# Projection and routing of a transformer layer on one core: modulation moved to ScalarE behind the transposition, and GpSimd's work put in another order

## The reference

```python
x = x + ga * attention(...)
h = _layernorm(x, axis=-1) * (1 + cb) + sb
logits = h @ gate_w.T
scores = sigmoid(logits)
topk_idx, topk_w = route_tokens(scores, bias_corr)
shared = relu2(h @ shared_up_w.T) @ shared_down_w.T
```

## Time and profile before

| what | value |
|---|---|
| median of 3 runs | 2968.14 us (2962.25 to 2969.26) |
| profiled execution, span from its first to its last instruction | 3027.5 us |
| mean granted clock of TensorE in it | 0.985 |
| PE busy | 2895.4 us, 96% |
| VectorE busy | 2179.3 us, 72% |
| GpSimd busy | 1833.5 us, 61% |
| ScalarE busy | 1341.6 us, 44% |

### The profile page before, as it was taken

One profiled execution on the slowest core, in us unless ns is written; L12 is line 12 of the kernel. 1 busy time (PEld: TensorE's weight loads), 2 busy tenths in 40 slices (PEclk: granted clock), 3 DMA queues, 4 the chain that ended last, 5 costly groups with the idle time before them and its releaser, 6 DMA issues.

```text
span 3027.5 us, 49806 instructions
## 1 busy us (share of the span) xinstructions
PE 2895.4 (96%) x16480; PEld 2168.3 (72%) x16480; DVE 2179.3 (72%) x5344; ACT 1341.6 (44%) x2436; POOL 1833.5 (61%) x1077
## 2 busy tenths in 40 slices
PE   8999999999999999999999989999999999989997
PEld 5788888766666666666666677777777787767775
DVE  6555555678787878787877687777777787756664
ACT  2222222156666666666666522233222333226664
POOL 1233222278888888888886256766565666655664
PEclk9999999999999999999999999999999999999998
DMA  7655555756655665566555333332322322238996
GB/s 240 211 187 201 187 180 180 233 114 136 137 124 115 138 138 121 115 139 140 119 117 160 107 97 93 94 112 74 103 79 93 102 85 81 73 107 222 239 245 118
DMA packets 281948, 420.53 MB, mean 139 GB/s; under 512 B 48463, under 2 KB 132687, under 8 KB 281742
## 3 DMA queue, kind: packets, MB, share of 16 engines
q1 hardware_dynamic: 259214, 384.22, 44.9%
q0 software_dynamic: 22528, 33.72, 5.8%
HBM read 263.38 MB, written 153.01 MB: 138 GB/s over the span
## 4 chain that ended last, share of the span: by engine, by line
PE 53%; DVE 14%; POOL 14%; issue 8%; ACT 4%; DMA 4%; another core or an unknown queue 2%; DVEq 1%; POOLq 0%; SPq 0%; ACTq 0%
PE qkv_ps_m L840 12%; PE ffn_ps_m L2191 11%; POOL att_gathered L1105 6%; PE qkv_ps_m L844 6%; POOL att_pt L1098 5%; PE att_ps_o L1330 5%; PE att_ps_p L1386 4%; PE att_ps_s L1304 4%; DMA out<-exp_y,exp_tok_add 2%; PE exp_ps_u L1607 2%; PE exp_ps_y L1623 1%; PE att_ps_s L1361 1%; DVE ffn_att L147 1%; DVE ffn_x L149 1%
## 5 line engine op out<-in xcount | busy, mean ns | idle before, releaser
L247 DVE CUSTOM_DVE_ANT_0 att_ps_s<-att_ps_s,att_causal 128x512 f32<-128x512 f32 (+1 forms) x992 | 469.3, 502 | 175.5 <-PE att_ps_s L1304 171.3
L1166 ACT ACTIVATE att_pt<-att_ps_p 128x512 f32<-128x512 f32 (+1 forms) x1024 | 524.5, 589 | 143.6 <-PE att_ps_p L1389 110.2
L1304 PE MATMUL att_ps_s<-att_ks,att_qs 96*128 96x512 f32 x1488 | 513.4, 373 | 2.2 <-DVE att_lower L253 0.6
L1386 PE MATMUL att_ps_p<-att_qs,att_ks 98*128 98x512 f32 (+3 forms) x1536 | 498.5, 364 | 9.3 <-ACT att_pt L1166 8.0
L1098 POOL TENSOR_TENSOR att_pt<-att_pt 128x1024 f32<-128x1024 f32 (+2 forms) x153 | 331.1, 2164 | 166.6 <-PE att_ps_o L1330 144.8
L1105 POOL TENSOR_TENSOR att_gathered<-att_gathered,att_pt 128x2048 f32<-128x2048 f32 (+1 forms) x92 | 388.1, 4218 | 7.2
L1912 POOL DMA_INDIRECT slot_info<-ffn_info,ffn_slot x256 | 275.9, 1078 | 119.3 <-issue 76.5
L253 DVE TENSOR_REDUCE att_lower<-att_ps_s 128x1 f32<-128x512 f32 x496 | 339.2, 684 | 7.4 <-PE att_ps_s L1304 7.4
L1386 PEld LDWEIGHTS att_ps_p<-att_qs,att_ks 98*128 98x128 f32 x1536 | 272.6, 191 | 82.1 <-issue 34.7
L1304 PEld LDWEIGHTS att_ps_s<-att_ks,att_qs 96*128 96x128 f32 x1488 | 275.7, 191 | 73.3 <-DVE att_rowmax L247 27.7
L577 POOL TENSOR_TENSOR qkv_x<-qkv_x,qkv_mod 128x512 f32<-128x512 f32 x60 | 83.4, 1391 | 371.5 <-DVE qkv_x L671 371.5
(11 more groups left out here) (311 smaller groups left out, 6718.8 us busy)
## 6 DMA issues: line engine op xcount, KB each, us to landing
att_qs<-qk_parts SPq DMA_DIRECT2D x96, 512.0 KB, 6.8
att_ks<-qk_parts SPq DMA_DIRECT2D x96, 512.0 KB, 12.7
qk_parts<-qkv_out_hi SPq DMA_DIRECT2D x128, 256.0 KB, 2.2
qk_parts<-qkv_out_lo SPq DMA_DIRECT2D x128, 256.0 KB, 2.4
qkv_x<-x SPq DMA_DIRECT2D x16, 1024.0 KB, 5.6
v_rows<-qkv_out_v SPq DMA_DIRECT2D x64, 256.0 KB, 2.3
att_vs<-v_rows SPq DMA_DIRECT2D x32, 512.0 KB, 16.1
o_parts<-att_o SPq DMA_DIRECT2D x64, 256.0 KB, 7.9
```

The lines of the kernel that those rows point to most:

```text
L247: dve.tensor_tensor_reduce(part, part, self.causal[:, UNIT - (c1 - c0):UNIT], scale=1.0, scalar=MASKED, op0=ALU.add, op1=ALU.max, accum_ou ...
L1166: act.activation(tile(c)[:, h, col:UNIT], ps_p[(NPROB * prev.g + n) % NP][:, col:UNIT], ACT.Exp, scale=float(HD) ** -0.5).then_inc(exp_don ...
L1304: pe.matmul(bank("s", cur.g, i)[:, 0:c1 - c0], qs[cur.slot][0:STACK, h, t * P:(t + 1) * P], ks[cur.slot][0:STACK, h, c0:c1], start=True, s ...
L1386: last = pe.matmul(part[:, i * (UNIT - col):(i + 1) * (UNIT - col)], ks[prev.slot][:, h + i, kt * P:(kt + 1) * P], qs[prev.slot][:, h + i, ...
```

## The change

- `turn` on PE transposes the normalised, not yet modulated h2 (it waits for norm_done). TURNS puts transpositions 0 and 1 after tile 1 of the down projection, 2 after tile 2, and 3 before pair 2 of tile 3 instead of before pair 4.
- ScalarE scales and shifts each transposed tile in its PSUM bank, in four instructions of 128x128 with a scale and a bias per partition, from a new buffer `mod_cols`, and takes the high part afterwards. Two DMAs of 512 single elements each fill `mod_cols`.
- GpSimd modulates all four tiles of h2 itself (for the store, which the experts' gathers read), each after its transposition. Its order becomes: wait for all four norms, `normalise`, then four times a modulation of one tile of u + 1 and four scatters of u.
- VectorE no longer modulates tile 3. `norm_first` takes two instructions a tile instead of three.
- SP stores h2 of unit u in body u instead of body u - 1, and loads the modulation rows and columns behind it, in odd bodies, ahead of attention's output.

```diff
             def norm_first():
...
                 for t in range(UT):
-                    last = dve.tensor_scalar(late.h2[:, t, :], late.x0[:, t, :], bridge.mv[:, t, 0:1], bridge.rstd[:, t:t + 1],
-                                             ALU.subtract, ALU.mult)
+                    dve.scalar_tensor_tensor(late.h2[:, t, :], late.x0[:, t, :], bridge.mv[:, t, 0:1], bridge.mod[:, 1, :],
+                                             op0=ALU.subtract, op1=ALU.mult).then_inc(late.mul_done, 1)
...
-        TURNS = ((), (0,), (1, 2), ())
-        SCATTERED_AHEAD = TOPK
+        TURNS = ((), (0, 1), (2,), ())
+        LAST_TURN = 2
...
             def load_mod(b):
...
+                for m, j in enumerate((M_CB, M_SB)):
+                    sp.dma_start(mod_cols[:, m, :], mod_dram[bass.ds(b, 1), j, :].rearrange("o (k p) -> p (o k)", p=P),
+                                 allow_slow_non_contiguous=True).then_inc(mod_in, 16)
...
             def store_h2(b, half):
                 u = b * HALVES + half
-                sp.wait_ge(h_done, CREDIT + PT * (u + 1))
-                sp.wait_ge(norm_done, CREDIT + UT * (u + 1))
+                sp.wait_ge(h_done, CREDIT + UT * (u + 1))
...
-                if more:
-                    nb, nhalf = (b, 1) if half == 0 else (b + 1, 0)
...
-                        sp.wait_ge(proj_done, CREDIT + UT * (u + 2))
-                        load_o(b + 1, half)
-                    store_h2(nb, nhalf)
-                    if half == 0 and has_next2:
-                        load_mod(b + 1)
+                if u and more:
+                    store_h2(b, half)
+                if more and half == 1:
+                    sp.wait_ge(hi_done, CREDIT + UT * (u + 1))
+                    load_mod(b + 1)
+                if b < LAST:
+                    sp.wait_ge(proj_done, CREDIT + UT * (u + 2))
+                    load_o(b + 1, half)
...
+            def modulate(u, t):
+                pool.wait_ge(tr_done, CREDIT + UT * u + t + 1)
+                ht = h2[:, t, :]
+                pool.tensor_tensor(ht, ht, mod[:, 1, :], ALU.mult).then_inc(mul_done, 1)
+                pool.wait_ge(mul_done, CREDIT + UT * u + t + 1)
+                pool.tensor_tensor(ht, ht, mod[:, 2, :], ALU.add).then_inc(h_done, 1)
...
             def body(b, half, more):
                 u = b * HALVES + half
-                if u == UNITS - 2:
-                    scatter(u, half, 0, SCATTERED_AHEAD)
-                if more:
-                    modulate(*((b, 1) if half == 0 else (b + 1, 0)))
-                if half == 0 and not (isinstance(b, int) and b == LAST) or half == 1 and more:
-                    normalise(u + 2)
-                scatter(u, half, SCATTERED_AHEAD if u == UNITS - 2 else 0, UT * TOPK)
+                if b < LAST:
+                    pool.wait_ge(norm_done, CREDIT + UT * (u + 1))
+                    normalise(u + 2)
+                if more:
+                    pool.wait_ge(mod_in, CREDIT + MOD_FIRST + MOD_EACH * ((u + 1) // HALVES + 1))
+                    pool.sem_inc(mark, 1)
+                for t in range(UT):
+                    if more:
+                        modulate(u + 1, t)
+                    scatter(u, half, t * TOPK, (t + 1) * TOPK)
...
             def turn(u):
+                if u:
+                    act.wait_ge(mod_in, CREDIT + MOD_FIRST + MOD_EACH * (u // HALVES + 1))
                 for t in range(UT):
                     act.wait_ge(tr_done, CREDIT + UT * u + t + 1)
+                    if u:
+                        for k in range(DK):
+                            part = ps_t[t % 2][:, k * P:(k + 1) * P]
+                            last = act.activation(part, part, ACT.Identity, bias=mod_cols[:, 1, k:k + 1], scale=mod_cols[:, 0, k:k + 1])
+                        last.then_inc(modulated, 1)
+                        act.wait_ge(modulated, CREDIT + UT * (u - 1) + t + 1)
...
             def attend(b, half):
...
-                dve.wait_ge(mod_in, CREDIT + 48 * (b + 2))
+                dve.wait_ge(mod_in, CREDIT + MOD_FIRST + MOD_EACH * (b + 1))
...
-                dve.tensor_tensor(h2[:, PT, :], h2[:, PT, :], mod[:, 1, :], ALU.mult).then_inc(dve_own, 1)
-                dve.wait_ge(dve_own, own + 2)
-                dve.tensor_tensor(h2[:, PT, :], h2[:, PT, :], mod[:, 2, :], ALU.add).then_inc(norm_done, 1)
...
             def turn(u, t):
-                if t < PT:
-                    pe.wait_ge(h_done, CREDIT + PT * u + t + 1)
+                if u:
+                    pe.wait_ge(norm_done, CREDIT + UT * (u - 1) + t + 1)
```

More of the change, by code:

```diff
@@ L131, in __init__ @@
         self.tr_done, self.hi_done, self.lo_done = s.sem("tr"), s.sem("hi"), s.sem("lo")
+        self.modulated = s.sem("modulated")
         self.cross_done, self.logit_done = s.sem("cross"), s.sem("logit")
@@ L197, in __init__ @@
         self.q_in, self.v_in, self.m_in = s.sems("q_in", SLOT), s.sems("v_in", SLOT), s.sems("m_in", SLOT)
-        self.pool_own, self.add_done, self.sum_done, self.mark = (s.sem(n) for n in ("pool_own", "add", "sum", "mark"))
+        self.pool_own, self.add_done, self.sum_done = (s.sem(n) for n in ("pool_own", "add", "sum"))
+        self.mark = late.mark
         self.s_done, self.max_done = s.sem("s"), s.sem("max")
@@ L1246, in normalise_first @@
                 dve.wait_ge(late.x_in[0], CREDIT + 16)
-                dve.wait_ge(late.mod_in, CREDIT + 48)
+                dve.wait_ge(late.mod_in, CREDIT + MOD_FIRST)
             def norm_first():
@@ L1711, in project_programs @@
         mul_done, h_done, proj_done, att_done = late.mul_done, late.h_done, late.proj_done, late.att_done
-        tr_done, hi_done, lo_done = late.tr_done, late.hi_done, late.lo_done
+        tr_done, modulated, hi_done, lo_done = late.tr_done, late.modulated, late.hi_done, late.lo_done
         cross_done, logit_done = late.cross_done, late.logit_done
@@ L1839, in load_experts @@
                     relay.load_up(sp, e, e, e_upT)
+                store_h2(LAST, 1)
                 for e in range(RELAY_RING):
@@ L1866, in gpsimd @@
             pool.iota(tok_i[:, :], pattern=[[P, UT]], base=0, channel_multiplier=1).then_inc(pool_own, 1)
-            def modulate(b, half):
-                u = b * HALVES + half
-                for t in range(PT):
-                    pool.wait_ge(norm_done, CREDIT + UT * u + t + 1)
-                    ht = h2[:, t, :]
-                    pool.tensor_tensor(ht, ht, mod[:, 1, :], ALU.mult).then_inc(mul_done, 1)
-                    pool.wait_ge(mul_done, CREDIT + PT * u + t + 1)
-                    pool.tensor_tensor(ht, ht, mod[:, 2, :], ALU.add).then_inc(h_done, 1)
+            def modulate(u, t):
[4 more added lines that the diff above has]
+                pool.tensor_tensor(ht, ht, mod[:, 2, :], ALU.add).then_inc(h_done, 1)
             def normalise(u):
@@ L2020, in attend @@
                 late.deviation(dve, u, LINKS * u, mv, std, rstd, tmp)
-                own += 2 * UT + 1 + STAT_LINKS + ROOT_LINKS
                 dve.wait_ge(tr_done, CREDIT + UT * u)
@@ L2287, in before_pair @@
                     def before_pair(n):
-                        if more and t == PT and 2 * n == UP:
+                        if more and t == PT and n == LAST_TURN:
                             turn(u + 1, PT)
```

37 lines of the change are left out of this document (9 added, 28 removed).

## The result

| | before | changed |
|---|---|---|
| median of the timed runs | 2968.7 us (2962.25 to 2974.15, 4 runs) | 3042.8 us (3035.88 to 3055.25, 4 runs) |
| ratio, 95% interval | | 1.0251 (1.0222 to 1.0279) |
| span of the profiled execution | 3027.5 us | 3053.5 us |
| unit 0's to unit 15's last gate matmul | 956.2 us | 975.5 us |
| predicted | | 2988 us, 2942 to 3020 |

The change costs 74 us, not 20. The time is outside the range, on the side that I had called likeliest. The first thing to see is that the two profiled executions differ by 26 us only.

A forecast was written before the change was run, and what follows sets the result against it. PE, nearly always busy in the stage, can win only time it stands still or runs slow. Terms -45.3 + 55 + 8 + 3 - 1 = +20 on the 3027.5 us span, less 59, gave 2988 us, range 2942 to 3020.

The forecast's parts named there:

- Waits removed: PE's transposition waits for GpSimd's shift and hT_lo: 33.4 us go, with 11.9 us of lower clock, -45.3 us.
- The odd bodies: Modulation rows load late, delaying VectorE's update and PE's transposition: 9.2 us in each of six bodies, +55 us.
- The lower clock: PE's granted clock falls after the idle stretch before the down projection in odd bodies: 1.1 us a body.
- Even bodies: GpSimd's modulations run beside VectorE's choose steps and last a_lo: 1 us on each of eight, +8 us.
- ScalarE: Four more 278 ns instructions a tile, covered by 4.1 us of matmuls: cost nothing, 15 us at the upper end.
- GpSimd: Timetable in a body: normalise ends +1.0, modulate(0) +4.1, slots about +5.0, last modulated tile +31 us.
- The first norms' -1: First norms in the last attention group take 8 instructions instead of 12, mostly under PE's work: -1 us.
- The tail: Last unit: scatter(14), now with modulations between its parts, ends beside VectorE's choose steps: +3 us (0 to 5).
- Faster: Rival: slots at +3, rows at +35.9, odd bodies cost only 29 us: -17, 2951 us; chance 0.2.
- about the same: Rival: load lands at +36 and the lower clock doesn't come: -5, 2963 us; chance 0.2.
- the main case: The forecast itself: mod_in complete at +39 in odd bodies, +20 us in all, 2988 us; chance 0.45.
- Slower still: Rival: column loads take 3 us, GpSimd's modulations stretch, odd bodies cost 77 us: +42, 3010 us; chance 0.15.

The follow-up runs named there:

- the version with everything together: Changed kernel with GpSimd's four modulations in one piece behind normalise, ahead of the sixteen scatters: 2961.0 us, ratio 0.9984; timed again later, 2984.2 us, 1.0016.
- the version with two buffers: Changed kernel with a second buffer for the ga row and the columns, loaded a body earlier; GpSimd's two rows stay behind the store: 2984.1 us, ratio 1.0065.
- session 1: First of three timing sessions; here the kernel before, unchanged and profiled again: 2963.2 us, ratio 0.9995.
- the late load alone: Kernel before with only the next batch's row loads moved to the odd body, behind the third projection tile: 3034.1 us, ratio 1.0214.

## Why the prediction was wrong, step by step

**The step that failed** is the first term, "Waits removed" with its clock, -45.3, together with the sentence that followed the sum: "the median of three runs is 2968.1, 59 us below that span, and I carry the difference over unchanged". The 59 us were not an offset that any kernel would show. They were for the most part those very waits and their clock: 54.4 of them lie in the stage, and the waits for GpSimd and hT_lo fall from 39.4 to 9.1 us. The sum removed 45 us of waits from the execution that had them, and then the 59 us took them away a second time. Against the profiled execution the forecast looks nearly right: +20 forecast, +26 measured (3053.5 - 3027.5), 3047 us where the median came out at 3042.8. That closeness is chance, since the second profile of the changed kernel has a span of 3037.7 us, which makes +10. The profile held the warning: a body without waits came out at 59.5 us, thirteen of them at 63, and a median 2% below the span leaves little room for 45 us of waits in ordinary executions. What removing the waits is worth there is 5.6 us, by the version with everything together. So the term was mis-sized: -45.3 put in, -5.6 measured.

**The odd bodies: right, each of them.** Forecast: last tile +31, update +39, transposition +53.0, 9.2 us each. Measured: +31.0, +40.4, +54.8 in body 5, and 68.48 - 59.23 = 9.25 us on average. Only the count was off: I left body 9 out because its issue waits would hide the load. Those waits belonged to the one execution too, and body 9 took 68.5 us like the rest. 7 x 9.25 = +65 instead of +55. The middle of that chain was right by luck in part: the columns cost about nothing (0.8 put in), and from the last tile to the update went 9.4 us instead of 7.9. The lower clock, put at 1.1 us a body, was less: an update at +31.0 would still have let PE transpose at +44.9, body 5's comes 9.4 us after that, and the body is 9.9 us longer, which leaves 0.5. The clock did fall as forecast: it is 0.51 from 2070 to 2080, and the matmuls follow each other every 0.43 us there. But at 0.227 us the 48 of the first two tiles would have ended at about 2085.8, 2 us before VectorE's first normalised tile (2087.44 and about 0.5), so most of what the clock takes lies where PE would have waited.

**Even bodies: +8 forecast.** Bodies 2 to 12 are 2.0 us longer each in the first profile (+12), body 14 +0.3, and body 0 3.2 shorter, since there PE no longer waits for GpSimd: +9 in all. (In the second profile the even bodies are 1.3 us longer.) The size per body was up to double my 1 us and the place was right. By the Trainium skill (SBUF — State Buffer, section "SBUF: two separate sides"), the one of the two that comes second to the shared ports, GpSimd or a VectorE instruction in a 2-port mode or with two inputs in SBUF, waits for the other's whole instruction. The rows of the version with two buffers agree in where the long ones end. The 128x4 instruction of 1.69 us ends at 1981.35, with GpSimd's of 1.30 (1981.31), and the a_lo of 1.48 us ends 0.56 us after GpSimd's of 1.70. The 128x4 one is listed as starting 0.35 us before GpSimd's, which the rule alone doesn't explain, and whether it runs in such a mode no row shows. In the changed kernel the mean a_lo of the stage is 1.09 us, against 0.71 in the kernel before (session 1).

**ScalarE: nothing, right; the price was not.** 433 ns each instead of 278, four in 1.48 us instead of 1.1. The earlier trace rows was a copy without a scale and a bias from SBUF. The Trainium skill (ScalarE: Activation LUTs, section "What ACT_TABLE_LOAD costs") gives 186 ns plus 0.833 ns an element and 93 ns for each operand that is read per partition, which by estimate is 479 for ours, with an overlap of 93 between two in a row, so 1.64 us for four; that is nearer to the measured 433 ns and 1.48 us than my row, and the upper end that I named was not needed.

**GpSimd: right.** Normalise ends at +1.9 (forecast +1.0), tile 0 at +4.5 (+4.1), the slots at +5.2 (+5.0), the last tile at +31.0 (+31). The first norms' -1 can't be told: body 0 begins at 1708.7 and 1699.4 us in the changed kernel, at 1709.0, 1710.2 and 1701.8 in the kernel before.

**The tail: +3 forecast.** The last unit's down projection starts at +27.0 in both profiles of the changed kernel, against +24.0 in the first session's profile of the kernel before; that is the 3 us forecast, but in the other two profiles of the kernel before it starts at +25.6 and +27.9. From the last gate matmul to the end go 369.3 and 364.2 us with the change, against 357.4, 359.0 and, in the shown profile, 362.3 without. So the tail costs 2 to 12 us, some of it in the experts, whose gathers and issue waits vary from one execution to the next. That part isn't settled.

The sum by what the runs show, against the profile of before in session 1: odd bodies +65, even ones with 0 and 14 +9, tail +12 is 86, and the stage begins 1.5 us sooner; the spans differ by 84.1 (3053.5 - 2969.4). The medians differ by 74, since the profiled execution of the changed kernel was the longest of its four, 12 us above their median. By its second profile the stage gives +72, the tail +7 and the start -11, and the spans differ by 68.

**The rivals.** "Faster" and "about the same" both rested on a load at +36; it came at +40, since modulate(0) and the slots took what the main case said. "Slower still" had the right side and the wrong reason: neither columns nor stretched modulations, but a smaller gain. My range stopped at 3020 because I let every case start from -45.3; no case asked whether the gain was there at all.

## What to carry to other kernels

Ahead of any sum, hold the span of the profiled execution against the median of the timed ones, and work out what a loop body takes without waits. If the span is 2% above the median, the waits that fill those 2% may not be there in ordinary executions, and removing them wins little, here 5.6 us instead of 45; cost the change against the clean body instead, where here 7 x 9.25 = 65 alone gives most of the 74. A second profile of the same kernel is the cheapest test. And when a producer that nobody waited for is spread out between other work, ask which buffer it holds until its last instruction, and which load stands behind that: here 20 us of lateness on an engine with time to spare became 9 us on the critical one, once per batch.

## What the runs showed of the hardware

- Executions of one kernel on one core differ by more than I had assumed, in the same stage: 901.8, 916.1 and 956.2 us in three profiles of the kernel before. The two of the changed kernel gave 975.5 and 974.1. The likely reason, argued and not tested, is that small delays before +31 vanish behind a wait that ends at +40.
- A load of 512 single elements, 4 bytes each, lands as fast as a row of 256 KB: the columns' line in the changed kernel (whole trace) gives

```profile
DMA to landing us min/median/max: 4.9/5.1/10.1
```

against 5.1/5.5/6.9 for the row loads of before. The Trainium skill (DMA: Bandwidth & Descriptors, "Rules for kernel authors") says that such a load becomes one descriptor per element; at 512 elements the most that a run shows for it is the 57.7 against 59.4 us of waits, 0.2 us a body.
- Three row loads right behind a 1 MB store on the same queue were used 9.0 us after the first issue, without a store ahead after 4.8; landing took 5.8 and 3.4 us (median).
- What a fall of the clock around a wait of PE costs depends on who is waited for next. Granted 0.51 from 2070 to 2080 in the changed kernel's body 5 left about 0.5 us, since VectorE was the later one. Granted 0.61 from 1953 to 1961 with the late load alone, it stood on the path, 17.2 us to the next gate matmul against 14.4.
